# Merging and moving the copies of the held lookups, and layer 3 with its weight column stationary, in a recommendation tower

## The chip, the cores and the metric

The kernel runs on one core of a Trainium2 chip. The metric is the device time of one execution in microseconds (us), lower is better. Three executions of the kernel before took 525.3, 527.55 and 530.39 us; the median is 527.55 us.

## The reference

2048 samples each have a dense vector of 128 numbers and 26 indices, one into each of 26 tables of 128-number rows. Per sample the 27 vectors (dense and 26 looked up) are multiplied with each other in all 351 pairs. The products and the dense vector go through three layers:

```python
e = jnp.stack([tbl_0[ids[:, 0]], ..., tbl_25[ids[:, 25]]], axis=1)
combined = jnp.concatenate([dense[:, None, :], e], axis=1)          # (2048, 27, 128)
z = jnp.einsum('bfd,bgd->bfg', combined, combined)[:, IU0, IU1]      # 351 pairs
h = jnp.concatenate([dense, z, dense], axis=1)                       # (2048, 607)
h = jnp.maximum(h @ W_top1 + b_top1, 0.0)                            # 512 wide
h = jnp.maximum(h @ W_top2 + b_top2, 0.0)                            # 256 wide
y = h @ W_top3                                                       # 1 wide
```

## The kernel before

**Tiling.** The samples are worked in 8 pairs of tiles, `i` = 0 to 7, with 128 samples in each tile (`a` = 0 and 1). `PAIR` is 256 samples. The looked-up vectors come in two ways.

- 17 tables are gathered with indirect DMAs that POOL issues (L341), in five groups of 4, 4, 4, 4 and 1 tables, numbered `q` = 0 to 4. TensorE transposes each group (`turn`, L369) into one of two PSUM banks `p_turn`. ScalarE (ACT) copies it into `feats[a]` (`keep`, L580), and its semaphore count lets later turns go on. After a turn POOL may gather the same group of the next pair.
- 9 small tables lie in SBUF, split into a high and a low part. VectorE (DVE) makes a one-hot matrix for 256 samples (`make_onehot`, L713, a ring of three), and 16 matmuls pick the rows (`select`, L411). The result has 256 columns, one half for each tile of the pair, in `p_sel`. `keep_selected` (L603) copies 128 columns for each tile into `feats[a]`.

**Held selections.** Four of the nine selections of the next pair (k = 0 to 3, `HELD`) are made early, during the second half of the pair before, and stay in PSUM: two in each bank of `p_sel`. They can only be copied out once all products that read the old `feats[1]` are done, so the first copy waits for the last bank of `gram(i-1, 1)`. Selection k = 4 needs bank 0 free, so it waits for the copies of k = 0 and 1.

**Products.** `gram` (L433) computes the pair products of a tile in four banks of 16 fp32 matmuls; each shows as two matmul records, so a bank is 32 records. ACT copies each bank to `prods` (`keep_prods`, L618). SP stores `prods` to a DRAM buffer `square` in four DMAs (L203), waits for them to land, and reads the upper half back as `pairs_h` (L214, L217), the input of layer 1 (L448 and L454). Layer 2 is L491, layer 3 L503. DVE adds the biases and clips (L718, L723) and copies layer 3's result (L730).

**Order of the work.** All orders are written out by hand, one instruction stream for each engine, tied by semaphores. In pair `i`, TensorE does `turn(i,0,q)` for q = 0 to 4, with the last products of the pair before after q = 0 and 1 (two banks each), and the remaining selections k = 4 to 8 spread over q = 2 to 4 by the function `selections`. Then it turns the second tile, between which layers 1 to 3 of pair i-1, the products of tile 0 and the held selections of pair i+1 are placed. For TensorE pairs 2 to 6 are a loop, 0, 1 and 7 are written out. A last part does the final tile's products and the layers of the last pair by tile.

**Results.** `y` holds 16 columns of 128 samples in SBUF, filled two columns a pair, and goes out in one DMA at the end (L327).

Of the kernel before, what the change touches and what calls it, by code (L numbers as in the profile page):

```python
# [14 lines left out]
C = F + 1  # L15
# [59 lines left out]
def selections(q, first, second):  # L75
# [5 lines left out]
    start = 1 if second else 2  # L81
# [6 lines left out]
def place(k, first):  # L88


    return (k // 2, k % 2) if k < HELD and not first else (k % 2, 0)


def program(nc, x_t, ids, ids_t, tables, w_dense, w_pairs, b1, w2, b2, w3, out):
    ctx = ExitStack()
    with ctx:
# [39 lines left out]
        y = sb("y", [T, B // T])  # L136
        spare = sb("spare", [128, VC * D])

# [55 lines left out]
        s_out = sem("s_out")  # L194
# [28 lines left out]
        def _(sp):  # L223
# [71 lines left out]

            def pair(i, b, first=False, second=False, last=False, late=False):
                more = not (last or late)
                if not first:
                    store(i - 1, 1, first=second)
                if more and not first:  # L300
                    load_ids_part(i + 2, b, 0)
# [23 lines left out]

            sp.wait_ge(s_yr, NP + 1)
            sp.dma_start(out, y[:, :]).then_inc(s_out, 16)  # L327
            sp.wait_ge(s_out, 16)
# [29 lines left out]
        def _(pe):  # L358
# [137 lines left out]
            def layer3(u, own):  # L496

                for a in range(own.start // T, own.stop // T):
                    for k in range(M2):
                        if a == own.start // T and (k == 0 or own.stop - own.start == T):  # L500

                            pe.wait_ge(s_h2r, M2 * u + (k + 1 if own.stop - own.start == T else M2))
                        mm = pe.matmul(p_mlp[:, a:a + 1], h2[:, k, a * T:a * T + T], w3s[:, k:k + 1],  # L503
                                       start=(k == 0), stop=(k == M2 - 1))
                mm.then_inc(s_y, 1)
# [67 lines left out]
        def _(act):  # L573
# [18 lines left out]
            def keep_selected(i, k, first=False):  # L592

                f = C - 1 - k
                if k == 0 and not first:

                    act.wait_ge(s_gram, NG * 2 * i)
# [6 lines left out]
                ins.then_inc(s_fsel, 1)  # L604

# [15 lines left out]
            def pair(i, first=False, second=False):  # L621
# [7 lines left out]
                for q in range(NQ):  # L629
# [41 lines left out]
        def _(dve):  # L671
# [54 lines left out]
            def result(u, tile, own):  # L726

                own = slice(own.start // T, own.stop // T)
# [96 lines left out]
```

## Time and profile before

| | |
|---|---|
| median of three executions | 527.55 us |
| the profiled execution's own time | 527.54 us |
| its span in the trace | 525.4 us |
| mean granted TensorE clock | 0.86 of full |
| TensorE matmuls busy | 398.8 us (76%) |
| TensorE weight loads busy | 357.2 us (68%) |
| POOL busy | 260.7 us (50%) |
| DVE busy | 204.2 us (39%) |
| ACT busy | 160.5 us (31%) |
| DMA | 43.88 MB, 84 GB/s on the mean |

The span is what the trace shows from the first to the last instruction; about 2.1 us of the execution's time lie outside it. A busy share is an average over stages with different limits; what one change is worth has to be read in the stage where it acts. "Remote" or "another core or an unknown queue" as the end of a wait means that a semaphore moved at that moment, though no record of an instruction ends there. This kernel has only one core, so in its trace it is always a queue or a delay that has no record.

### The profile page before, as it was taken

The page shows a single profiled execution, that of the slowest core. Times are in us where ns is not written, and L with a number is a line of the kernel's source. Part 1 is how long each engine was busy: PE and PEld are TensorE (multiplying, and loading weights), DVE is VectorE, ACT ScalarE, POOL GpSimd, SP SyncE. Part 2 cuts the span into 40 slices and gives each one's busy share as a digit, 9 for nine tenths or more (in the row PEclk, how much of TensorE's full clock was granted, in tenths as well). Part 3 has the DMA queues.
Part 4 walks back from the last instruction along what each step waited for, and adds up shares of the span by engine and source line. Part 5 has one row for each costly group of instructions (what it writes and reads, how often), then busy time and mean ns, then how long its engine had stood idle before and what let it go on. Part 6 is the DMA issues. An engine that isn't in the chain of part 4 may idle for free.

```text
span 525.4 us, 9717 instructions
## 1 busy us (share of the span) xinstructions
PE 398.8 (76%) x3968; PEld 357.2 (68%) x3968; DVE 204.2 (39%) x157; ACT 160.5 (31%) x314; POOL 260.7 (50%) x278
## 2 busy tenths in 40 slices
PE   3641947674697689966897789955897588979997
PEld 2530846564586588955886578945886587868887
DVE  6110935553233434450533434450533532545103
ACT  0000543262222244214422333214421432226330
POOL 6774765645435654555546654565445653540000
PEclk9965877887898779978899679986999778979999
DMA  8981221743313152314414161313414140222031
GB/s 212 260 274 30 86 62 40 174 81 107 131 29 79 41 129 78 72 47 92 118 35 77 45 155 45 66 51 65 144 36 77 40 100 25 47 45 55 3 58 28
DMA packets 66355, 43.88 MB, mean 84 GB/s; under 512 B 51713, under 2 KB 56408, under 8 KB 66204
## 3 DMA queue, kind: packets, MB, share of 16 engines
q1 hardware_dynamic: 56068, 25.48, 20.1%
q0 software_dynamic: 8704, 17.84, 13.3%
q10 hardware_dynamic: 1560, 0.24, 0.3%
q8 instruction: 16, 0.26, 0.2%
q14 instruction: 7, 0.06, 0.0%
HBM read 37.78 MB, written 5.76 MB: 83 GB/s over the span
## 4 chain that ended last, share of the span: by engine, by line
PE 54%; another core or an unknown queue 26%; issue 7%; ACT 7%; DMA 3%; DVE 1%; ACTq 1%; SPq 1%; DVEq 0%
PE p_sel L411 24%; PE p_gram L433 9%; PE p_mlp L454 7%; PE p_turn L369 5%; PE p_mlp L491 3%; ACT feats L603 3%; ACT feats L580 3%; PE p_mlp L448 2%; DMA dense<-in_x_t 2%; PE p_sel L381 2%; ACT prods L618 1%; DMA square<-prods 1%; PE p_mlp L503 1%; DMA pairs_h<-square 1%
## 5 line engine op out<-in xcount | busy, mean ns | idle before, releaser
L341 POOL DMA_INDIRECT rows<-in_table,index x272 | 260.1, 956 | 208.2 <-PE p_turn L369 79.5
L713 DVE TENSOR_TENSOR onehot<-ids_all,p_rows 128x2048 fp32r<-128x2048 int32 x72 | 163.0, 2283 | 156.6 <-PE p_sel L411 83.8
L411 PE MATMUL p_sel<-onehot,high 125*128 125x256 f32 x528 | 153.4, 322 | 41.3 <-ACT feats L603 33.1
L411 PE MATMUL p_sel<-onehot,low 125*128 125x256 f32 x528 | 146.0, 308 | 1.8 <-issue 1.8
L411 PEld LDWEIGHTS p_sel<-onehot,high 125*128 125x128 f32 x528 | 114.9, 218 | 45.8 <-issue 25.6
L411 PEld LDWEIGHTS p_sel<-onehot,low 125*128 125x128 f32 x528 | 115.1, 218 | 3.2 <-issue 2.9
L580 ACT ACTIVATE feats<-p_turn 128x512 f32<-128x512 f32 (+1 forms) x80 | 79.6, 996 | 87.5 <-PE p_turn L369 49.2
L433 PEld LDWEIGHTS p_gram<-feats 128*54 128x54 f32 x2048 | 71.8, 156 | 50.5 <-issue 38.6
L433 PE MATMUL p_gram<-feats 128*54 128x52 f32 x2048 | 80.6, 241 | 33.1 <-ACT feats L580 17.3
L603 ACT ACTIVATE feats<-p_sel 128x128 f32<-128x128 f32 x144 | 44.6, 443 | 112.3 <-remote 65.5
L618 ACT ACTIVATE prods<-p_gram 118x416 f32<-118x416 f32 x64 | 33.4, 522 | 134.0 <-remote 93.7
L369 PE MATMUL p_turn<-ident,rows 128*128 128x128 f32 x272 | 51.5, 309 | 13.5 <-issue 13.5
L369 PEld LDWEIGHTS p_turn<-ident,rows 128*128 128x128 f32 x272 | 35.3, 157 | 17.2 <-issue 15.1
L454 PE MATMUL p_mlp<-pairs_h,weights 117*128 117x256 f32 x168 | 42.6, 391 | 0.0
L718 DVE TENSOR_SCALAR h<-p_mlp,b1s 128x256 f32<-128x256 f32 x28 | 13.5, 483 | 73.7 <-PE p_mlp L454 73.7
L454 PEld LDWEIGHTS p_mlp<-pairs_h,weights 117*128 117x128 f32 x168 | 33.0, 197 | 4.9
L491 PE MATMUL p_mlp<-h,weights 128*128 128x256 f32 x112 | 26.6, 380 | 0.2 <-DVE pairs_h L723 0.2
L381 PE MATMUL p_sel<-onehot,weights 125*128 125x256 f32 x48 | 13.5, 441 | 11.4 <-issue 11.4
L491 PEld LDWEIGHTS p_mlp<-h,weights 128*128 128x128 f32 x112 | 20.2, 190 | 2.6 <-issue 0.4
L723 DVE TENSOR_SCALAR pairs_h<-p_mlp,b2s 128x256 f32<-128x256 f32 x14 | 6.8, 484 | 35.1 <-remote 24.9
L381 PEld LDWEIGHTS p_sel<-onehot,weights 125*128 125x128 f32 x48 | 10.7, 225 | 13.4 <-issue 11.6
L448 PE MATMUL p_mlp<-dense,weights 128*128 (+1 forms) x56 | 17.4, 393 | 0.0
(46 smaller groups left out, 124.8 us busy)
## 6 DMA issues: line engine op xcount, KB each, us to landing
ids_all<-in_ids_t SPq DMA_DIRECT2D x25, 256.0 KB, 4.7
square<-prods SPq DMA_DIRECT2D x62, 87.8 KB
rows<-in_table,index POOLq DMA_INDIRECT x272
pairs_h<-square SPq DMA_DIRECT2D x14, 117.0 KB
weights<-in_table SPq DMA_DIRECT2D x3, 448.0 KB
prods<-in_table SPq DMA_DIRECT2D x3, 448.0 KB
ids_all<-in_ids_t SPq DMA_DIRECT2D x1, 1152.0 KB
ids_all<-in_ids_t SPq DMA_DIRECT2D x6, 128.0 KB
```

Of the source, the lines that this page charges most:

```text
L341: pool.indirect_dma_start(out=rows[a][:, f, :], out_offset=None, in_=tables[f], in_offset=bass.IndirectOffsetOnAxis(ap=index[:, (2 * i + a ...
L369: mm = pe.transpose(p_turn[(NQ * a + q) % 2][:, k * T:k * T + T], rows[a][:, f, :], ident[:, :])
L381: mm = pe.matmul(p_sel[k % 2][:, 0:PAIR], piece[k][0:VP, c, :], onehot[k % RING][0:VP, c, :].bitcast(F32), start=(c == 0), stop=(c == VC - 1))
L411: mm = pe.matmul(p_sel[bank][:, half * PAIR:half * PAIR + PAIR], part[k][0:VP, c, :], hot, start=(c == 0 and part is high), stop=(c == VC ...
L433: mm = pe.matmul(p_gram[b % 2][WIDE * tile:WIDE * tile + BLK, BLKC * k:BLKC * k + BLKC], group, feats[a][:, GB * b + k, js, 1:C], start=Tr ...
L448: pe.matmul(bank1(m, False)[:, 0:PAIR], wdense[:, cols], dense[:, bass.ds(i * PAIR, PAIR)], start=True, stop=False)
L454: mm = pe.matmul(bank1(m, False)[:, 0:PAIR], wpairs[:, c, cols], pairs[:, c, :], start=False, stop=(c == NCH - 1))
L491: mm = pe.matmul(bank2(m, tail)[:, 0:own.stop - own.start], w2s[:, k, 128 * m:128 * m + 128], h1[:, k, own], start=(k == 0), stop=(k == M1 ...
L580: nc.scalar.activation(dst, src, ACT.Copy).then_inc(s_feats, 1)
L603: ins = nc.scalar.activation(feats[a][:, :, :, f].rearrange("d g j -> d j g"), src, ACT.Copy)
L618: nc.scalar.activation(prods[a][0:RISE, :, GB * b:GB * b + GB], src, ACT.Copy)\
L713: nc.vector.tensor_tensor(onehot[k % RING][:, :, :], at, of, ALU.is_equal).then_inc(s_onehot, 1)
```

## The change

There are three edits.

1. **Selections and turns.** In pairs 2 to 7 the selections k = 4 to 8 start one group later (`start = 3` instead of 2): TensorE turns groups 2 and 3 back to back, then does k = 4 and 5, turns group 4, then k = 6 to 8.
2. **Copies of the held selections.** The two selections of a bank lie in swapped halves (`1 - k % 2`), so that their order in the bank is their order in `feats`, and one ACT instruction copies 2 x 128 columns of a tile. A bank takes two instructions (`keep_held`) instead of four. The copies of bank 0 now come before the copy of the last bank of products, and those of bank 1 right behind it, both ahead of group 2's copy.
3. **Layer 3.** The weight column `w3s` is the stationary operand and `h2` the moving one, so the result is one row of 256 numbers on one partition. `y` becomes a ring of two such rows in the memory of `spare`. SP stores each row when it is two pairs old (`store_y`), and DVE waits for that store before it writes the row again.

```diff
-    start = 1 if second else 2
+    start = 1 if second else 3
...
-    return (k // 2, k % 2) if k < HELD and not first else (k % 2, 0)
+    return (k // 2, 1 - k % 2) if k < HELD and not first else (k % 2, 0)
...
-        y = sb("y", [T, B // T])
         spare = sb("spare", [128, VC * D])
+        y = spare[0:1, 0:2 * PAIR]
...
+            def store_y(u, half):
+
+                sp.wait_ge(s_yr, u + 1)
+                sp.sem_inc(s_passed, 1)
+                sp.dma_start(out[:, bass.ds(u * PAIR, PAIR)], y[:, half * PAIR:half * PAIR + PAIR]).then_inc(s_out[half], 16)
...
                 if not first:
                     store(i - 1, 1, first=second)
+                if not (first or second):
+                    store_y(i - 2, b)
                 if more and not first:
                     load_ids_part(i + 2, b, 0)
...
-                for a in range(own.start // T, own.stop // T):
-                    for k in range(M2):
-                        if a == own.start // T and (k == 0 or own.stop - own.start == T):
-
-                            pe.wait_ge(s_h2r, M2 * u + (k + 1 if own.stop - own.start == T else M2))
-                        mm = pe.matmul(p_mlp[:, a:a + 1], h2[:, k, a * T:a * T + T], w3s[:, k:k + 1],
-                                       start=(k == 0), stop=(k == M2 - 1))
+                for k in range(M2):
+                    if k == 0 or own.stop - own.start == T:
+
+                        pe.wait_ge(s_h2r, M2 * u + (k + 1 if own.stop - own.start == T else M2))
+                    mm = pe.matmul(p_mlp[0:1, own], w3s[:, k:k + 1], h2[:, k, own],
+                                   start=(k == 0), stop=(k == M2 - 1))
...
+            def keep_held(i, bank):
+
+                f = C - 2 - 2 * bank
+                if bank == 0:
+
+                    act.wait_ge(s_gram, NG * 2 * i)
+                act.wait_ge(s_sel, SEL * i + 2 * bank + 2)
+                held = p_sel[bank].rearrange("d (f a j g) -> d f a j g", f=2, a=2, j=4)
+                for a in range(2):
+                    dst = feats[a][:, :, :, f:f + 2].rearrange("d g j f -> d f j g")
+                    ins = nc.scalar.activation(dst, held[:, :, a, :, :], ACT.Copy)
+                ins.then_inc(s_fsel, 2)
...
                     if not (first or second) and q < 2:
-                        keep_prods(i - 1, 1, range(NH * q, NH * q + NH))
-                    if not first and q == (0 if second else 1):
-                        for k in range(HELD // 2):
-                            keep_selected(i, k)
+                        keep_prods(i - 1, 1, (NH * q,))
+                        if q == 1:
+                            keep_held(i, 0)
+                        keep_prods(i - 1, 1, (NH * q + 1,))
+                        if q == 1:
+                            keep_held(i, 1)
+                    if second and q == 0:
+                        keep_held(i, 0)
                     if second and q == 0:
                         high_bits(5)
-                    if not first and q == (1 if second else 2):
-                        for k in range(HELD // 2, HELD):
-                            keep_selected(i, k)
+                    if second and q == 1:
+                        keep_held(i, 1)
...
-                nc.vector.tensor_copy(y[:, bass.ds(tile, own.stop - own.start)], p_mlp[:, own])\
+                nc.vector.tensor_copy(y[:, half * PAIR + own.start:half * PAIR + own.stop], p_mlp[0:1, own])\
                          .then_inc(s_yr, 1)
```

**How the instructions move.** ACT, in the loop over the pairs, from the last two copies of products (L618 before, L639 now; the held copies are L603 before and L624 now, a group's copy L580 and L591). Before:

```order
L618 ACTIVATE prods<-p_gram 118x52x8
L616 REGISTER_ALU
L618 ACTIVATE prods<-p_gram 118x52x8
L597 REGISTER_ALU
L598 ISA
L603 ACTIVATE feats<-p_sel 128x4x32 x2
L598 REGISTER_ALU
L603 ACTIVATE feats<-p_sel 128x4x32 x2
L577 REGISTER_ALU
L580 ACTIVATE feats<-p_turn 128x4x4x32
L598 REGISTER_ALU
L603 ACTIVATE feats<-p_sel 128x4x32 x2
```

Now:

```order
L639 ACTIVATE prods<-p_gram 118x52x8
L619 REGISTER_ALU
L620 ISA
L624 ACTIVATE feats<-p_sel 128x2x4x32 x2
L637 REGISTER_ALU
L639 ACTIVATE prods<-p_gram 118x52x8
L620 REGISTER_ALU
L624 ACTIVATE feats<-p_sel 128x2x4x32 x2
L588 REGISTER_ALU
L591 ACTIVATE feats<-p_turn 128x4x4x32
L588 REGISTER_ALU
L591 ACTIVATE feats<-p_turn 128x4x4x32
```

The first held copies went ahead of the last copy of products, and the copies of groups 2 and 3 now stand together.

TensorE, in its loop, from the last bank of products to group 4's single transpose. Before (the turns are L369, the selections L411):

```order
L433 MATMUL p_gram<-feats 54x52 x16
L367 REGISTER_ALU
L369 MATMUL p_turn<-ident,rows 128x128 x4
L393 REGISTER_ALU
L406 REGISTER_ALU
L411 MATMUL p_sel<-onehot,high 128x256
...
L367 REGISTER_ALU
L369 MATMUL p_turn<-ident,rows 128x128 x4
L393 REGISTER_ALU
L400 REGISTER_ALU
L411 MATMUL p_sel<-onehot,high 128x256
```

Now (the turns are L381, the selections L423):

```order
L445 MATMUL p_gram<-feats 54x52 x16
L379 REGISTER_ALU
L381 MATMUL p_turn<-ident,rows 128x128 x4
L379 REGISTER_ALU
L381 MATMUL p_turn<-ident,rows 128x128 x4
L405 REGISTER_ALU
L418 REGISTER_ALU
L423 MATMUL p_sel<-onehot,high 128x256
```

The turn of group 3 left its place between selections 4 and 5 and stands ahead of selection 4.

SP, in its loop: one DMA of 256 numbers is put between the four stores of products and the next load of indices.

```order
 L203 DMA square<-prods 702x1x32 x4
+L300 ISA
+L300 DMA out_y<-spare 1x256
 L238 ISA
 L241 ISA
```

Everything that SP issues behind it, the read-back of the products first, has one more DMA ahead of it in the queue.

## Rows read from the trace of the kernel before

**Rows 1.** The page, the chain that ended last, shares by engine.
```profile
PE 54%; another core or an unknown queue 26%; issue 7%; ACT 7%; DMA 3%; DVE 1%; ACTq 1%; SPq 1%; DVEq 0%
```

**Rows 2.** Stretches of pairs 2 to 7: length, busy us by engine, clock, DMA.
```profile
core 0: us, PE busy (x) PEld busy (x) DVE busy (x) ACT busy (x) POOL busy (x), PEclk, DMA share, GB/s
169.77:200.70 30.93, 22.12 (x227) 20.73 (x228) 12.09 (x7) 11.92 (x30) 16.98 (x18) 0.77 0.38 96
229.24:259.82 30.58, 23.67 (x236) 21.81 (x237) 12.26 (x7) 11.99 (x31) 16.97 (x18) 0.79 0.37 89
287.81:319.17 31.36, 24.22 (x227) 22.14 (x228) 12.09 (x7) 12.16 (x30) 16.98 (x18) 0.69 0.39 94
347.67:378.43 30.76, 21.78 (x227) 20.42 (x228) 12.04 (x7) 12.06 (x31) 16.97 (x18) 0.78 0.37 96
407.03:438.69 31.66, 22.54 (x226) 21.19 (x227) 12.20 (x7) 12.38 (x30) 16.99 (x18) 0.77 0.26 60
468.10:487.98 19.88, 18.32 (x227) 17.59 (x228) 11.32 (x6) 12.46 (x31) 0.94 (x1) 0.85 0.20 41
```

**Rows 3.** ACT's timeline in pair 5: start, us, line, [idle before it <- releaser].
```profile
362.15 0.52 ACT L618 ACTIVATE prods<-p_gram 118x416 f32<-118x416 f32 x1 [4.62 <-remote]
362.56 1.09 ACT L603 ACTIVATE feats<-p_sel 128x128 f32<-128x128 f32 x4
363.42 1.16 ACT L580 ACTIVATE feats<-p_turn 128x512 f32<-128x512 f32 x1
364.36 1.16 ACT L603 ACTIVATE feats<-p_sel 128x128 f32<-128x128 f32 x4
367.52 0.64 ACT L603 ACTIVATE feats<-p_sel 128x128 f32<-128x128 f32 x2 [1.99 <-PE p_sel L411]
...
374.80 0.63 ACT L603 ACTIVATE feats<-p_sel 128x128 f32<-128x128 f32 x2 [3.77 <-PE p_sel L411]
```

**Rows 4.** TensorE's timeline, the turn of group 2 in pair 5.
```profile
358.25 0.66 PE L369 MATMUL p_turn<-ident,rows 128*128 128x128 f32 x4
```

**Rows 5.** TensorE's timeline, the first matmul of selection 4 in pairs 2 to 6.
```profile
185.84 0.58 PE L411 MATMUL p_sel<-onehot,high 125*128 125x256 f32 x1 [4.68 <-ACT feats L603]
...
242.49 0.58 PE L411 MATMUL p_sel<-onehot,high 125*128 125x256 f32 x1 [3.00 <-ACT feats L603]
...
301.00 0.58 PE L411 MATMUL p_sel<-onehot,high 125*128 125x256 f32 x1 [2.14 <-ACT feats L603]
...
363.70 0.58 PE L411 MATMUL p_sel<-onehot,high 125*128 125x256 f32 x1 [4.79 <-ACT feats L603]
...
420.23 0.58 PE L411 MATMUL p_sel<-onehot,high 125*128 125x256 f32 x1 [3.02 <-ACT feats L603]
```

**Rows 6.** The chain in order of time: start, us, what.
```profile
363.70 3.78 PE p_sel L411 x16
367.48 0.85 PE p_turn L369 x4
...
488.15 1.30 PE p_mlp L454 x6
```

**Rows 7.** SP's timeline, reading back products: pair 5, then pair 7.
```profile
368.92 2.31 SPq L214 DMA_DIRECT2D pairs_h<-square  x3
...
481.61 2.25 SPq L214 DMA_DIRECT2D pairs_h<-square  x3
483.91 0.48 SPq L217 DMA_DIRECT2D pairs_h<-square  x1
```

**Rows 8.** Groups by line and form: busy us, mean ns of one, idle before.
```profile
L503 PE MATMUL p_mlp<-w3s,pairs_h 128*128 128x1 f32 x64 | 8.9, 256 | 10.9 <-issue 5.8 <-DVE pairs_h L723 5.2
L723 DVE TENSOR_SCALAR pairs_h<-p_mlp,b2s 128x256 f32<-128x256 f32 x14 | 6.8, 484 | 35.1 <-remote 24.9 <-PE p_mlp L491 10.2
L730 DVE COPY y<-p_mlp 128x2 f32 x4 | 0.6, 160 | 12.7 <-PE p_mlp L503 7.2 <-remote 5.5
```

**Rows 9.** DVE's timeline at the end of the program.
```profile
522.50 0.35 DVE L723 TENSOR_SCALAR pairs_h<-p_gram,b2s 128x128 f32<-128x128 f32 x1 [0.54 <-PE p_gram L491]
...
523.33 0.16 DVE L730 COPY y<-p_mlp 128x1 f32<-128x1 f32 x1 [0.47 <-PE p_mlp L503]
```

More of the change, by code:

```diff
@@ L193, in program @@
         s_yr = sem("s_yr")
-        s_out = sem("s_out")
+        s_out = [sem(f"s_out{half}") for half in range(2)]
         s_passed = sem("s_passed")
@@ L324, in _ @@
             read_back(NP - 1, (1,), chunks=(0, 1))
+            store_y(NP - 2, NP % 2)
             sp.wait_ge(s_yr, NP + 1)
-            sp.dma_start(out, y[:, :]).then_inc(s_out, 16)
-            sp.wait_ge(s_out, 16)
+            last = (NP - 1) % 2 * PAIR
+            sp.dma_start(out[:, B - PAIR:B], y[:, last:last + PAIR]).then_inc(s_out[(NP - 1) % 2], 16)
+            for half in range(2):
+                sp.wait_ge(s_out[half], 8 * NP)
         @block.gpsimd
@@ L594, in keep_selected @@
                 f = C - 1 - k
-                if k == 0 and not first:
-                    act.wait_ge(s_gram, NG * 2 * i)
                 act.wait_ge(s_sel, SEL * i + k + 1)
@@ L724, in relu2, with result @@
                                         b2s[:, m:m + 1], 0.0, ALU.add, ALU.max).then_inc(s_h2r, 1)
-            def result(u, tile, own):
-                own = slice(own.start // T, own.stop // T)
+            def result(u, half, own, stored=None):
+                if stored is not None:
+                    dve.wait_ge(s_out[half], 16 * stored)
                 dve.wait_ge(s_y, u + 1)
-                nc.vector.tensor_copy(y[:, bass.ds(tile, own.stop - own.start)], p_mlp[:, own])\
+                nc.vector.tensor_copy(y[:, half * PAIR + own.start:half * PAIR + own.stop], p_mlp[0:1, own])\
                          .then_inc(s_yr, 1)
@@ L744, in _, with pair @@
                 split_low(k)
-            def pair(i, b, second=False, last=False):
+            def pair(h, b, second=False, last=False, stored=True):
+                i = 2 * h + b
                 own = slice(0, PAIR)
@@ L768, in pair @@
                         make_onehot(i + 1, 1 - b, HELD - 1)
-                result(i - 1, 2 * (i - 1), own)
+                result(i - 1, 1 - b, own, h - 1 + b if stored else None)
             for k in range(HELD):
@@ L774, in _ @@
                 split_low(k)
-            pair(1, 1, second=True)
-            with dve.Fori(1, NP // 2 - 1) as h:
+            pair(0, 1, second=True, stored=False)
+            pair(1, 0, stored=False)
+            pair(1, 1)
+            with dve.Fori(2, NP // 2 - 1) as h:
                 for b in range(2):
-                    pair(2 * h + b, b)
-            pair(NP - 2, 0)
-            pair(NP - 1, 1, last=True)
+                    pair(h, b)
+            pair(NP // 2 - 1, 0)
+            pair(NP // 2 - 1, 1, last=True)
             for a in range(2):
@@ L786, in _ @@
                     relu2(NP - 1 + a, own, m, tail=True)
-                result(NP - 1 + a, 2 * (NP - 1) + a, own)
+                result(NP - 1 + a, (NP - 1) % 2, own, (NP - 1) // 2)
 def kernel(**inputs):
@@ L818 @@
           for k, a in arrays.items()}
-    out = nc.dram_tensor("out_y", (T, B // T), F32, kind="ExternalOutput").ap()
+    out = nc.dram_tensor("out_y", (1, B), F32, kind="ExternalOutput").ap()
     program(nc, ap["in_x_t"], ap["in_ids"], ap["in_ids_t"], [ap[f"in_table_{n}"] for n in range(F)],
@@ L823 @@
     r = run_bass_kernel_spmd(nc, [arrays], core_ids=[0])
-    return np.ascontiguousarray(r.results[0]["out_y"].T).reshape(B, 1)
+    return np.ascontiguousarray(r.results[0]["out_y"]).reshape(B, 1)
```

## The prediction, made before the changed kernel ran

> **What bounds the kernel now.** I read the chain that ended last first. TensorE holds 54% of it and ACT 7%, but 26% goes to "another core or an unknown queue" [rows 1]. With one core that can only be hidden waits: a semaphore moves late though no record ends there. So the kernel is bound by TensorE's order of work with its hand-overs, and a quarter of the chain is time that no instruction's record explains.
>
> Next I cut out the stage that the change touches. It runs from ACT's copy of group 4 of the second tile, after which the products of pair i-1 go on, to ACT's first copy of the second tile of pair i. The table of stretches has it for pairs 2 to 7 [rows 2]. In the loop pairs 2 to 6 it takes 30.93, 30.58, 31.36, 30.76 and 31.66 us, in pair 7, with the same work but no gathers (POOL 0.94 us busy against 17 us), 19.88 us. So some 11 us of each loop stretch are hidden waits or lower clock, and they are there only while POOL gathers. The five loop stretches differ by at most 1.1 us.
>
> The start of selection 4 in them is the most telling row [rows 5]. Counted from the stretch's start [rows 2], it comes at 16.07 us in pair 2 (185.84 - 169.77), 13.25 in pair 3, 13.19 in pair 4, 16.03 in pair 5 and 13.20 in pair 6. From there to the stretch's end it takes 14.86, 17.33, 18.17, 14.73 and 18.46 us. Pairs that start selection 4 2.8 us earlier get nothing for it: the rest grows by 2.5 to 3.7 us. The reader is to see that a head start before selection 4 has so far been taken back by a hidden wait behind it, such as the one before ACT's copy at 374.80 [rows 3].
>
> **The change part by part.**
>
> *Copies of the held selections.* Before, ACT copies the last bank of products at 362.15, the held bank 0 from 362.56 to 363.65, and selection 4 starts at 363.70 behind it [rows 3, 5]. Now bank 0 goes first, so it is free 0.41 us earlier (362.56 - 362.15). The merge itself I cost at nothing. Four copies of 128 columns take 363.42 - 362.56 = 0.86 us until the next instruction begins, and one copy of 512 takes 364.36 - 363.42 = 0.94 us [rows 3]. The same 512 columns cost the same in four instructions as in one, so two of 256 lie between, at 0.9 us.
>
> The Trainium skill says otherwise (VectorE: DVE Perf Modes, The TRN2 errata): each ScalarE instruction from PSUM pays 172 cycles at 1.2 GHz beside its columns, and few large ones are to be used. By that, an estimate, a bank would fall from 1.00 us (4 x 300 cycles) to 0.71 us (2 x 344), which gives 0.29 us more on the path of each pair, 1.7 us over six. The rows speak for no such gain, and the sum goes by them.
>
> So this part is worth 0.41 us in each of pairs 2 to 7, if it is kept. In the five loop pairs rows 5 say that a head start of 2.8 us is not kept, so I take 0 of 2.05 us there (both ends stay in the range). What it costs: the last bank of products is copied some 0.9 us later, and SP's stores with it; see the read-back below. The copies of bank 1 now stand ahead of group 2's copy, which delays that by 0.9 us. It is needed for group 4's turn, 8 us later, so nothing waits for it.
>
> *Turn of group 3 ahead of selection 4.* Before, TensorE turns group 2 at 358.25 to 358.91 and has nothing until 363.70 [rows 4, 5]. The turn of group 3 stands between selections 4 and 5 and takes 0.85 us of the chain (367.48 to 368.33) [rows 6]. It needs only the copy of group 1, long made, and rows gathered a pair ahead. So now it lies in the idle 4.8 us, and selection 5 follows 4 at once: 0.85 us less work behind selection 4. In the five loop pairs that is 4.25 us. Bounds: 0, if the hidden wait takes it as it took the head start, and 0.85 us a pair plus more, since POOL may gather group 3 earlier. I take the 0.85: this is TensorE work removed from behind selection 4, not an earlier start of it, and rows 5 say nothing against that kind. ACT has more to do before its copy of selection 4, about 0.9 + 0.4 + 0.9 + 0.9 + 0.9 = 4.1 us from the last gram bank (a held bank, a product bank, a held bank, two groups), while selection 4 ends 0.9 + 3.78 = 4.7 us after it [rows 3, 6]. So that copy is not late.
>
> *Pair 7.* Here there is hardly a hidden wait. Both parts would give some 0.8 us (0.41 and about 0.44, the turn at full clock being half of the 0.85). But layer 1 must find the products read back. SP issues that read-back at 481.61 to 484.39 [rows 7] and layer 1's matmuls on it start at 488.15 [rows 6], 3.8 us later, landing included. The read-back moves 0.9 us later with the product copy and could just become the last to arrive. I take 0.4 us.
>
> *Layer 3.* Each fp32 matmul shows as two records. Before it is 8 records a pair, starting about 0.12 us apart (1 column moved, 128 loaded). Now it is 4 records of 256 columns. The other fp32 matmuls of 256 columns start 0.217 us apart (1.30 us for six) [rows 6], so 0.87 us stands against 0.96. 0.1 us a pair less, and it ends beside ACT's late copy of group 4, so I take 0 of 0.7 us.
>
> *Result copy.* 128 x 2 takes 160 ns; a DVE operation with 256 columns from PSUM takes 484 ns [rows 8]. That is 0.32 us more a pair. Behind it on DVE is the one-hot of selection 4, made in 2.3 us some 13 us before it is needed: hidden. If that cover were gone it would be 2.3 us over 7 pairs. In the tail the last copy lies on the path: 0.35 us for 128 columns against 0.16 [rows 9], +0.19 us.
>
> *Stores of y.* One DMA of 1 KB a pair, issued by SP between the stores of products and the index loads. SP's issues cost 0.77 us each (2.31 us for three) [rows 7]. After the stores SP waits for them to land before the read-back, and this gap takes one more issue, so 0. Without the gap it would push the read-back by 0.77 us. SP's and DVE's new waits are for things 40 us or more old. The final DMA is 1 KB instead of 8 KB: 0.
>
> *Sum.* -4.25 - 0.4 + 0.19 = -4.46 us. The profiled execution took 527.54 us (span 525.4 and 2.1 around it), which is the median shown. 527.54 - 4.46 = **523.1 us**.
>
> **The rivals.**
>
> *All is kept, and more.* If the hidden waits are a fixed addition, each loop pair also keeps the 0.41 us (2.05 in all), pair 7 its other 0.4 and layer 3 its 0.1 a pair: 523.1 - 3.1 = **520.0 us**. POOL's earlier gathers can add to it. For it speaks that each hand-over is on the chain; against it rows 5.
>
> *All is taken back.* The loop stretches all end within 1.1 us of each other whatever happens in them [rows 2]. If something outside TensorE's order sets the hidden wait's end (gathers, stores or index loads, which pair 7 lacks), the 4.25 us come back as a longer wait: 527.54 - 0.4 + 0.19 = **527.3 us**. For it speaks that 2.8 us were taken back; against it that the hidden wait differs from pair to pair.
>
> *Slower: the read-back becomes the last to arrive.* The product copy is 0.9 us later, the y store adds 0.77 us in SP's queue if landing is shorter than now, and layer 1 is wanted up to 1.3 us earlier, so the read-back comes up to 3.0 us closer to its use. In pair 5 its first three issues end at 371.23 [rows 7], 7.2 us before the stretch's end at 378.43, in pair 7 it is 4.1 us (483.86 to 487.98). Taking 3.8 us as an upper bound of what it needs (pair 7, where it was in time), pair 5 has 3.4 us to spare. It decides from a shift above that. Should the hidden waits lengthen it so that each of the 6 pairs waits 1.5 us, the gain of 4.46 is lost and 9 us come on top: 523.1 + 4.5 + 9 = 536; with half of it, **532 us**. Little speaks for it in the loop.
>
> **How the numbers follow.** What a measurement of this kernel can tell from no change is about 1%, 5.3 us: faster means below 522.3, slower above 532.8. I give the forecast (523.1, with 2.5 us to either side) 0.38, all kept 0.22, all taken back 0.30, slower mechanism 0.10. Faster by over 1%: nearly all of the second case and four in ten of the first, 0.36. Slower by over 1%: somewhat over half of the last, 0.06. Within 1%: 0.58. The range takes in the kept case with POOL's extra down to 518.5, and the case taken back with the runs' own spread up to 529.5.
>
> **What would show it.** (1) In the stretches of rows 2, 0.8 us less in pairs 2 to 6 and some 0.4 less in pair 7. (2) TensorE turns group 3 within 1 us behind group 2, and selection 5 begins at selection 4's end. (3) ACT's two held copies of a bank take 0.85 to 0.95 us to the next instruction; 0.7 would show the page right. (4) Selection 4 starts 1.1 us instead of 1.55 us after the last gram bank is seen by ACT. (5) The result copy takes about 0.48 us, with no wait of SP or DVE for the y stores. Stretches still at 30.6 to 31.7 us with a longer idle time ahead of ACT's copies of selections 5 or 6 would show the gain taken back; a wait of layer 1 for the read-back would show the slower case. The prediction is wrong altogether if the hidden waits change by microseconds, which no row here explains.

## The result, and the profile after

The changed kernel is slower. Four executions took 541.26 to 548.08 us, median 544.89, beside 528.25 us for the kernel before (525.3 to 530.39, four executions). The ratio is 1.032, with a 95% interval of 1.023 to 1.040. The forecast was 523.1 us with a range up to 529.5, so the result lies outside it, on the other side of no change. The comparisons leave disturbed executions out. The profile below is of the slowest of the four, 548.08 us, with a span of 546.3 us.

The chain that ended last, shares by engine, of the changed kernel:

```profile
PE 48%; another core or an unknown queue 27%; issue 9%; ACT 8%; DMA 4%; SPq 1%; DVE 1%; ACTq 1%; DVEq 0%
```

TensorE's share fell from 54% to 48% [rows 1]. In microseconds the hidden waits went from 0.26 x 525.4 = 137 to 0.27 x 546.3 = 147, and "issue" (an engine that waits for nothing the trace shows) from 37 to 49. TensorE itself went from 284 to 262. All shares are rounded, and one point is 5 us. TensorE had no less to do: its matmuls are busy for 403.4 us, beside 398.8 before. So some 22 us left TensorE's part of the chain, and hidden waits and "issue" grew by some 23.

The same six stretches as [rows 2], cut at the same two copies of ACT:

```profile
core 0: us, PE busy (x) PEld busy (x) DVE busy (x) ACT busy (x) POOL busy (x), PEclk, DMA share, GB/s
173.49:207.64 34.15, 24.66 (x227) 23.28 (x228) 12.18 (x7) 11.70 (x27) 16.99 (x18) 0.70 0.34 87
236.16:270.15 33.99, 21.89 (x227) 20.82 (x228) 12.17 (x7) 11.87 (x26) 16.99 (x18) 0.80 0.33 87
298.66:335.32 36.66, 23.22 (x233) 20.57 (x232) 12.07 (x7) 12.07 (x26) 16.99 (x18) 0.73 0.32 80
362.15:399.09 36.94, 25.27 (x227) 23.48 (x228) 12.17 (x7) 12.13 (x26) 16.97 (x18) 0.68 0.33 82
427.61:460.90 33.29, 23.03 (x227) 21.44 (x228) 12.17 (x7) 12.01 (x26) 16.97 (x18) 0.74 0.25 57
489.26:507.05 17.79, 16.97 (x227) 16.25 (x227) 11.49 (x6) 12.20 (x27) 0.94 (x1) 0.91 0.21 45
```

The six together take 192.8 us against 175.2, which is 17.6 of the 20.9 us between the two spans. The five loop stretches are 1.6 to 6.2 us longer each, with nearly the same busy times of ACT, DVE and POOL. Pair 7, which has no gathers, got 2.1 us shorter, at a granted clock of 0.91 instead of 0.85. Where did the loop's time go? ACT's timeline in pair 5, the place of [rows 3]:

```profile
377.29 0.52 ACT L639 ACTIVATE prods<-p_gram 118x416 f32<-118x416 f32 x1 [7.55 <-remote]
378.12 1.12 ACT L624 ACTIVATE feats<-p_sel 128x256 f32<-128x256 f32 x2 [0.31 <-PE p_gram L445]
379.02 0.57 ACT L639 ACTIVATE prods<-p_gram 118x416 f32<-118x416 f32 x1
379.48 1.11 ACT L624 ACTIVATE feats<-p_sel 128x256 f32<-128x256 f32 x2
...
391.65 0.64 ACT L611 ACTIVATE feats<-p_sel 128x128 f32<-128x128 f32 x2 [7.69 <-remote]
392.07 0.45 ACT L591 ACTIVATE feats<-p_turn 128x128 f32<-128x128 f32 x1
392.31 0.69 ACT L611 ACTIVATE feats<-p_sel 128x128 f32<-128x128 f32 x2
```

TensorE meanwhile, first the turns, then the last two matmuls it did before the wait, and the first one behind it:

```profile
377.93 1.97 PE L381 MATMUL p_turn<-ident,rows 128*128 128x128 f32 x8
...
385.01 0.27 PE L381 MATMUL p_turn<-ident,rows 128*128 128x128 f32 x1
...
386.90 0.28 PE L423 MATMUL p_sel<-onehot,low 125*128 125x256 f32 x1
392.44 0.55 PE L423 MATMUL p_sel<-onehot,high 125*128 125x256 f32 x1 [5.26 <-ACT feats L611]
```

The turns of groups 2 and 3 stand together (x8), as the order says. Selection 5 ended at 385.2, group 4's turn at 385.3, selection 6 at 387.2. ACT takes up all three from 391.65 on, as if their signals came in one lot, 6.5 us late for the first. DVE starts its next one-hot at 391.65 too, after its own hidden wait of 6.07 us. And TensorE stands still for 5.26 us, since selection 7 needs the bank that ACT had not emptied. POOL's timeline shows what ran beside it, the first and last of a burst of eight indirect gathers, 1.25 us apart, and the next gather:

```profile
379.86 0.94 POOL L353 DMA_INDIRECT rows<-in_table,index  x1 [4.37 <-PE p_turn L381]
...
388.59 0.94 POOL L353 DMA_INDIRECT rows<-in_table,index  x1 [0.30 <-issue]
392.46 0.94 POOL L353 DMA_INDIRECT rows<-in_table,index  x1 [2.93 <-remote]
```

ACT goes on 2.1 us after the burst ends (391.65 - 389.53, the last gather's end, 388.59 + 0.94). So it is in every loop pair of the changed kernel: ACT's wait behind selection 4 ends 2.0, 2.1, 2.8, 2.1 and 1.2 us after a burst of 8, 8, 12, 8 and 8 gathers. The burst has this form because the turns of groups 2 and 3 now end together and free eight gathers at once; in pair 4 the four of group 1 ran into them. The kernel before, same engine, pair 5:

```profile
366.72 0.94 POOL L341 DMA_INDIRECT rows<-in_table,index  x1 [0.30 <-issue]
369.14 0.94 POOL L341 DMA_INDIRECT rows<-in_table,index  x1 [1.48 <-issue]
```

There the turns lay on both sides of selection 4, and so there were two bursts of four with a pause of 1.5 us. That was so in pairs 2 and 5; in pairs 3, 4 and 6 a burst of eight ran beside or right behind selection 4. These are the very pairs whose rest behind selection 4 was 17.3 to 18.5 us instead of 14.8 [rows 2, 5]. In the changed kernel selection 4 starts here in pairs 2, 3 and 6 (TensorE's timeline):

```profile
189.25 0.58 PE L423 MATMUL p_sel<-onehot,high 125*128 125x256 f32 x1 [3.59 <-ACT feats L624]
...
251.91 0.58 PE L423 MATMUL p_sel<-onehot,high 125*128 125x256 f32 x1 [4.03 <-ACT feats L624]
...
443.35 0.58 PE L423 MATMUL p_sel<-onehot,high 125*128 125x256 f32 x1 [3.13 <-ACT feats L624]
```

Counted from the stretch's start that is 15.8, 15.7 and 15.7 us, and the rest takes 18.4, 18.2 and 17.5. So these pairs now have the late start of the one kind (16.0 before) and the long rest of the other (17.3 to 18.5). Before, each pair had only one of the two.

The kernel before had such waits too, at another place: ahead of group 4's copy of the second tile, where the stretches of [rows 2] start. ACT waits there for 6.8 to 7.4 us in four of the six. In pair 2 a burst of eight gathers ends at 167.61, and ACT goes on 2.2 us later:

```profile
169.77 0.40 ACT L580 ACTIVATE feats<-p_turn 128x128 f32<-128x128 f32 x1 [7.41 <-remote]
```

So a wait of this size beside eight gathers could be read from the trace before the change, just outside the stretches that were cut out.

Layer 3 and the result copy, now (busy us, mean ns, idle before); then the tail's result copy:

```profile
L514 PE MATMUL p_mlp<-pairs_h,w3s 128*1 128x256 f32 x28 | 7.9, 410 | 8.2 <-issue 4.4 <-DVE pairs_h L747 3.8
L756 DVE COPY spare<-p_mlp 1x256 f32<-1x256 f32 x7 | 2.9, 412 | 30.4 <-remote 20.2 <-PE p_mlp L514 10.2
```

```profile
544.40 0.28 DVE L756 COPY spare<-p_mlp 1x128 f32<-1x128 f32 x1 [0.54 <-PE p_mlp L514]
```

Pair 7, SP's last read-back and the layer 1 that uses it:

```profile
502.88 2.29 SPq L214 DMA_DIRECT2D pairs_h<-square  x3
505.21 0.48 SPq L217 DMA_DIRECT2D pairs_h<-square  x1
```

```profile
508.93 1.56 PE L466 MATMUL p_mlp<-pairs_h,weights 117*128 117x256 f32 x6 [1.71 <-DMA pairs_h<-square]
```

Layer 1 waits 1.71 us for the read-back, which it did not before [rows 6, 7].

### The profile page after: what moved, and what is told of

Its sections match the earlier page's. It is cut to its first block, busy times and chain, and to the rows that moved or that the text cites. A ratio compares the mean times of both kernels' runs of the same rounds, so it can differ in the third digit from the quotient of the medians.

```text
span 546.3 us, 9595 instructions
## 1 busy us (share of the span) xinstructions
PE 403.4 (74%) x3940; PEld 355.6 (65%) x3940; DVE 205.8 (38%) x157; ACT 159.1 (29%) x286; POOL 259.5 (48%) x278
## 3 DMA queue, kind: packets, MB, share of 16 engines
q0 software_dynamic: 8704, 17.84, 12.7%
## 4 chain that ended last, share of the span: by engine, by line
PE 48%; another core or an unknown queue 27%; issue 9%; ACT 8%; DMA 4%; SPq 1%; DVE 1%; ACTq 1%; DVEq 0%
PE p_sel L423 18%; PE p_gram L445 10%; PE p_mlp L466 7%; PE p_turn L381 5%; ACT feats L591 4%; PE p_mlp L503 4%; PE p_mlp L460 2%; DMA dense<-in_x_t 2%; PE p_sel L393 2%; ACT feats L611 1%; DMA square<-prods 1%; DMA pairs_h<-square 1%; ACT prods L639 1%; ACT feats L624 1%
## 5 line engine op out<-in xcount | busy, mean ns | idle before, releaser
L423 PE MATMUL p_sel<-onehot,high 125*128 125x256 f32 x528 | 157.2, 327 | 56.7 <-ACT feats L611 31.0
L423 PEld LDWEIGHTS p_sel<-onehot,high 125*128 125x128 f32 x528 | 118.7, 225 | 60.5 <-issue 47.1
L423 PE MATMUL p_sel<-onehot,low 125*128 125x256 f32 x528 | 150.2, 314 | 0.6 <-issue 0.4
L423 PEld LDWEIGHTS p_sel<-onehot,low 125*128 125x128 f32 x528 | 118.5, 225 | 2.2 <-issue 1.9
L445 PE MATMUL p_gram<-feats 128*54 128x52 f32 x2048 | 81.5, 236 | 39.3 <-issue 27.2
L591 ACT ACTIVATE feats<-p_turn 128x512 f32<-128x512 f32 (+1 forms) x80 | 78.6, 999 | 86.3 <-PE p_turn L381 52.9
L639 ACT ACTIVATE prods<-p_gram 118x416 f32<-118x416 f32 x64 | 33.6, 525 | 131.0 <-remote 84.8
L611 ACT ACTIVATE feats<-p_sel 128x128 f32<-128x128 f32 x88 | 28.7, 438 | 122.9 <-remote 82.8
L381 PE MATMUL p_turn<-ident,rows 128*128 128x128 f32 x272 | 49.8, 307 | 12.6 <-issue 12.6
L381 PEld LDWEIGHTS p_turn<-ident,rows 128*128 128x128 f32 x272 | 34.7, 155 | 18.0 <-issue 15.0
L624 ACT ACTIVATE feats<-p_sel 128x256 f32<-128x256 f32 x28 | 15.7, 671 | 16.6 <-remote 16.0
```

The lines of the kernel that those rows point to most:

```text
L381: mm = pe.transpose(p_turn[(NQ * a + q) % 2][:, k * T:k * T + T], rows[a][:, f, :], ident[:, :])
L423: mm = pe.matmul(p_sel[bank][:, half * PAIR:half * PAIR + PAIR], part[k][0:VP, c, :], hot, start=(c == 0 and part is high), stop=(c == VC ...
L445: mm = pe.matmul(p_gram[b % 2][WIDE * tile:WIDE * tile + BLK, BLKC * k:BLKC * k + BLKC], group, feats[a][:, GB * b + k, js, 1:C], start=Tr ...
L591: nc.scalar.activation(dst, src, ACT.Copy).then_inc(s_feats, 1)
L611: ins = nc.scalar.activation(feats[a][:, :, :, f].rearrange("d g j -> d j g"), src, ACT.Copy)
L639: nc.scalar.activation(prods[a][0:RISE, :, GB * b:GB * b + GB], src, ACT.Copy)\
```

## The experiments

A "loop pair" below is the time from one copy of group 4 of the second tile to the next, in pairs 2 to 6. It is 58.6 to 61.1 us in the kernel before and 61.6 to 65.5 in the changed one.

### Which edit costs?

`e1_turns_only`: the kernel before with

```diff
-    start = 1 if second else 2
+    start = 1 if second else 3
```

> The kernel before with edit 1 alone (selections 4 to 8 one group later, turns of groups 2 and 3 back to back). Theory A (turns back to back let POOL issue eight gathers in one burst while selections 4 and 5 hand over, and TensorE's signals reach the others only at its end): carries most of the loss, 1.02 to 1.035 of before, with bursts of eight gathers in every loop pair and ACT's copy of selection 5 about 2 us after their end. Theory B (the copies or their order slow the stretch): about 1.00. Theory C (the result ring, its stores and waits): 1.00.

`e2_copies_and_layer3`: the changed kernel's other two edits, with `start` as before.

> The changed kernel with edit 1 undone (edits 2 and 3 alone). Theory A: 0.99 to 1.005 of before. Theory B or C: 1.02 to 1.035. Layer 3 and the result copy should be worth less than 0.5%.

`e3_after_pool_holds_group3` (on the changed kernel) and `e4_before_pool_holds_group3` (on the kernel before), the same three lines, so that the burst is parted:

```diff
+                            if a == 0 and q == 3 and i > 2:
+                                pool.wait_ge(s_sel, SEL * (i - 1) + 7)
+                                pool.sem_inc(s_passed, 1)
```

> The changed kernel; POOL alone is altered: it holds back the gathers of group 3 of the first tile (pairs 2 on) until selection 6 of the pair is done, so that the burst of eight is broken up. Theory A: the idle time ahead of ACT's copy of selection 5 falls from about 7 to under 4 us, and the time falls to 0.99 to 1.015 of before. Theories B and C: unchanged at about 1.03, or slower since POOL is held.

> The kernel before with the same hold of POOL. Before has bursts of eight in pairs 3, 4 and 6 only. Theory A: those pairs' stretches lose 2 to 3 us each, 0.98 to 0.995 of before. Otherwise 1.00, or slower since POOL starts four gathers later.

Measured, all four on one chip with the kernel before at 526.92 us: e1 543.97 us, ratio 1.027 (1.021 to 1.033). e2 544.61 us, 1.033 (1.029 to 1.037). e3 536.45, 1.020 (1.014 to 1.027). e4 537.78, 1.017 (1.013 to 1.022).

The turns alone cost as much as the whole change, and the two other edits alone do too, where theory A had them at nothing. The effects do not add up. In e1, ACT's wait behind selection 4 is 5.2 to 7.8 us in the five loop pairs, behind or beside bursts of eight and twelve. In e2 it is 5.7 to 5.9 us in pairs 3 to 5, the three that take 62.9 to 63.7 us (pairs 2 and 6 take 60.0 and 59.4), and there is no burst of eight there: two bursts of four, 0.9 to 1.2 us apart instead of 1.5. So eight gathers without a pause are not needed for the wait.

With POOL held (e3), the wait goes where the burst is parted. In pair 2 nothing hidden is left ahead of selection 5's copy:

```profile
196.78 0.67 ACT L614 ACTIVATE feats<-p_sel 128x128 f32<-128x128 f32 x2 [2.15 <-PE p_sel L426]
```

The idle time ahead of that copy is 1.9 us in pairs 3 and 5 and 2.8 in pair 6; in pair 4, where a burst of eight came about all the same, 4.8. The part of the pair up to group 4's copy of the first tile gets shorter (21.8 to 23.5 us instead of 26.7 to 29.9), and the rest longer (35.6 to 40.3 instead of 34.9 to 35.9). The gathers have to be made some time, and their cost moves with them. Nor does the time show a gain: e3's 1.020 is less than the 1.032 of the result, but the changed kernel itself had 1.017 on this chip at another time (e7 below). And the kernel before loses by the same hold. So the burst explains the place of the wait; that it explains the loss is not shown.

The two halves of e2, on another chip, whose times were unsteady: the kernel before took 518.46 to 538.93 us there, median 529.98. `e14_layer3_only` has edit 3 alone, `e15_copies_only` edit 2 alone.

> The kernel before with edit 3 alone (layer 3, ring of results, stores pair by pair). If any small shift of the work against the gathers costs: 1.005 to 1.035. If only the copies and turns do: 0.995 to 1.005.

> The kernel before with edit 2 alone (held copies merged and put ahead). Edits 2 and 3 together measured 1.033: this one takes what the run with edit 3 alone does not show, 1.00 to 1.03.

e14 took 528.66 us (518.41 to 530.48), like the kernel before. e15 took 535.77 (532.52 to 541.68). Layer 3 costs nothing that can be told; the copies seem to cost about 1% by the medians, 2.7% between the fastest executions, which four of each can't bound.

`e7_after_again` and `e8_before_on_this_chip` are the two kernels unchanged.

> The changed kernel once more, beside before on one chip. In the run without gathers, before itself took 380 us on the chip it was given, against 527 us elsewhere. If this call gets a chip of the 527 us kind: 1.025 to 1.04. If it gets one of the 380 us kind, where the hidden waits are missing, the forecast's own terms stand alone: 0.98 to 0.995. If the loss came from the change's order itself it would be slower on both.

> The kernel before, for a profile beside the others of this call. On a chip of the 380 us kind: no waits that end by remote over 2 us in pairs 2 to 6, stretches of 18 to 21 us, gathers at the same 1.25 us apart or faster. On one of the 527 us kind: stretches of 30 to 32 us as before.

e7 took 542.72 us, ratio 1.017 (1.008 to 1.025) to a kernel before of 532.34 us; e8, one execution, 527.34. The change is slower again, by a size that differs from chip to chip and time to time: 1 to 4% hold all of it.

### What makes the hidden waits?

`e5_after_no_gathers` and `e6_before_no_gathers` leave out the gathers of pairs 2 to 7 in either kernel, so the rows of pair 1 are used again.

```diff
-                        for f in quad:
+                        for f in quad if i < 2 else ():
```

> The changed kernel without the gathers of pairs 2 to 7 (left out with TensorE's waits on them; the rows of earlier pairs are used again). Theory A: the hidden waits go altogether, loop stretches of 17.5 to 21 us as in pair 7 instead of 33 to 37 us, time 0.80 to 0.88 of before. If the waits come from something else (instruction supply, the loop, the stores): stretches stay over 28 us.

> The kernel before without the gathers of pairs 2 to 7, in the same way. Theory A: like the changed kernel without them, and slower than that by 4 to 12 us, the forecast's terms (0.41 + 0.85 us a pair) and what pair 7 gained. If the order itself costs time: faster than the changed kernel without gathers.

e5 took 379.39 us and e6 377.97. But the kernel before itself took 380.12 us on that chip (376.59 to 383.29, 19 executions), with all its gathers. So these two told nothing of what the gathers cost on the chips above, and something else: there are chips on which the kernel before loses hardly anything by them (e6 has 0.997 of its time, 0.993 to 1.000). Theory A had e6 slower than e5 by 4 to 12 us. It was the faster, by 1.4. The stretch of [rows 2] takes 17.5 us in e5's loop pairs and 18.0 in e6's, so the change gains 0.5 us there, and the rest of the pair 24.1 to 24.5 us against 23.7, so it loses more behind it. Even without a gather the change is no gain. The next two were run on a chip where the kernel before takes 532.34 us.

`e10_pool_fills_no_dma`: the kernel before; in pairs 2 to 7 POOL fills the rows by memsets, without a DMA. `e11_plain_dmas_from_pool`: the same bytes come by plain DMAs that POOL issues. Neither gives the looked-up rows.

```diff
                         for f in quad:
+                            if i >= 2:
+                                pool.dma_start(out=rows[a][:, f, :], in_=tables[f][0:128, :]).then_inc(s_rows[a][q], 16)
+                                continue
```

> The kernel before; in pairs 2 to 7 each gather is replaced by eight POOL memsets of 16 columns of the same rows (about 0.9 us, no DMA). If POOL's instructions as such hold TensorE's signals back: like before on this chip. If it is the indirect DMAs, or their traffic: 0.71 to 0.75 of before on a chip of the 527 us kind (380 us); 1.00 on one of the other kind.

> The kernel before; in pairs 2 to 7 each gather is replaced by a plain DMA of 128 rows in a row of the same table, issued by POOL: same bytes, no index. If the traffic or POOL's part in issuing a DMA holds the signals back: within 3% of before on this chip. If it is the indirect form (128 descriptors from an index): 0.71 to 0.85 of before on a chip of the 527 us kind.

e10 took 420.65 us, ratio 0.792 (0.785 to 0.798), e11 425.13 (420.62 and 429.63). Every loop pair takes 41.7 to 42.5 us instead of some 60, and ACT has no hidden wait left in pairs 2 to 7 (those up to 106 us, in the first two pairs with their gathers, stay). In e11 the same queue moves the same 8704 packets and 17.84 MB as before. So neither POOL's being busy nor the traffic as such makes the hidden waits; something that comes with the indirect form does. A plain DMA differs from a gather in more than one way: it reads no index, its rows lie in a row, and it takes POOL 0.53 us instead of 0.94 and 0.30 of pause. Which of these counts was not tried.

`e12_after_plain_dmas` and `e13_before_plain_dmas`: the same replacement in both kernels, on the unsteady chip above.

> The changed kernel; in pairs 2 to 7 each gather is replaced by a plain DMA of the same bytes from POOL, as done to the kernel before. Theory A (the change loses only by what the indirect gathers do to the hand-overs): 0.98 to 1.00 of the kernel before with plain DMAs in the same call, with 0.4 to 1.3 us less a pair. Rival (the change's order costs by itself): 1.005 to 1.03 of it.

> The kernel before with plain DMAs in pairs 2 to 7, timed again beside the changed kernel with them. 0.79 to 0.82 of before on a chip of the 527 us kind, with pairs of 41 to 43 us.

e12 took 432.7 us (427.66 to 436.83), e13 425.11 (420.83 to 429.03). Without hidden waits in the loop the change is still no gain; it seems to lose 7.6 us by the medians, and 4.9 between the two profiled executions (427.66 and 422.77). One row of the waits of each (us in total, times, longest) shows where, e12 first:

```profile
PE p_mlp L469 <- DMA pairs_h<-square: 9.6, 6, 2.7
```

```profile
PE p_mlp L457 <- DMA pairs_h<-square: 0.9, 1, 0.9
```

In all six pairs layer 1 now waits for the read-back of the products.

### Does the number of gathers count, or their density?

`e16_before_spaced_gathers` puts eight small memsets between the kernel before's gathers, from pair 2 on. `e17_before_half_gathers` makes only the first two of each group of four (`quad[:2]`), so the other rows keep old values. `e18_after_once_more` is the changed kernel.

```diff
+                            if i >= 2:
+                                for n in range(8):
+                                    ins = nc.gpsimd.memset(gap[:, 96 * (f % 4) + 12 * n:96 * (f % 4) + 12 * n + 12], 0.5)
```

> The kernel before, with eight small memsets on POOL ahead of each indirect gather from pair 2 on, which puts about 0.35 us between gathers; all gathers are still made. If it is the density of a burst that delays TensorE's signals, the hidden waits shrink and the loop pairs fall from about 59.5 us towards 55, the whole by 10 us or more, to below 517 us. If each indirect gather delays them by itself, the sum is the same or a little larger (POOL needs 34 x 1.6 = 54 us a pair, below 59.5): 525 to 540 us.

> The kernel before, which from pair 2 on gathers only the first two tables of each group of four (18 of 34 gathers a pair); the other rows keep old values. If the delay goes with the number of indirect gathers, a loop pair takes 41.7 + 18/34 x 17.8 = 51 us, the whole about 480 us. If it is a matter of long bursts (eight and twelve in a row), bursts of two and four leave little of it: a pair below 46 us, the whole below 455.

> The changed kernel as it is, beside runs of the kernel before on the same chip. On a chip where the kernel before takes about 527 us: 537 to 548 us. On one where it takes about 380 us, the indirect gathers delay nothing, so the two kernels differ as they do without gathers: 378 to 382 us.

They came to another chip of the undelayed kind: the kernel before took 379.97 us (376.33 to 384.31, 13 executions). So the question stays open. e17 took 378.66 us, 0.998 (0.995 to 1.002). e16 took 431.89, 1.140 (1.131 to 1.148), and its chain has another head than all others:

```profile
POOL 52%; PE 24%; issue 9%; DMA 7%; DVE 4%; SPq 2%; ACT 1%; ACTq 0%; POOLq 0%; DVEq 0%
```

A gather with its pause takes 1.535 us there, 34 of them 52.2 us, and the loop pairs after the first take 51.3 to 53.9. POOL is the bound. Without the pause it is 34 x 1.25 = 42.5 us, and e18's loop pairs take 42.8 to 42.9 (44.9 in pair 6): POOL has next to nothing to spare.

e18 took 386.7 us (384.89 to 389.89), ratio 1.017 (1.009 to 1.026), where I had expected 378 to 382. This run has no hidden wait at all, so the loss can be looked for in plain waits. The chain of e18, then that of e6, the order of before on such a chip, though without gathers:

```profile
PE 61%; DMA 17%; SPq 9%; issue 5%; DVE 4%; ACT 3%; ACTq 1%; DVEq 0%
```

```profile
PE 79%; DMA 7%; DVE 4%; issue 4%; ACT 3%; SPq 2%; ACTq 1%; DVEq 0%
```

DMA and SP's queue went from 9% to 26% of it; in e17, which has the order of before and half the gathers on e18's own chip, they hold 11%. SP's timeline of one pair in e18, and TensorE's:

```profile
248.42 3.54 SPq L203 DMA_DIRECT2D square<-prods  x4
252.24 0.36 SPq L300 DMA_DIRECT2D out_y<-spare  x1
252.97 0.37 SPq L241 DMA_DIRECT2D ids_all<-in_ids_t  x1
254.91 2.32 SPq L214 DMA_DIRECT2D pairs_h<-square  x3
```

```profile
257.84 0.60 PE L381 MATMUL p_turn<-ident,rows 128*128 128x128 f32 x4
258.28 0.60 PE L460 MATMUL p_mlp<-dense,weights 128*128 x2
260.21 1.56 PE L466 MATMUL p_mlp<-pairs_h,weights 117*128 117x256 f32 x6 [1.33 <-DMA pairs_h<-square]
```

The last bank of products is copied later, behind the held bank, so the stores end later and the read-back starts later, while layer 1 is wanted no later. e18 loses 9.6 us in six such waits, e5 (no gathers) 2.4 in five, e17 0.4 in one. In e17's pair 5 the read-back starts 12.4 us after the stretch's start, in e18's 13.7. With all gathers the kernel before has no profile on such a chip, so how much of the 9.6 us it has too is not known.

SP's timelines of e6 and e5 at the same pair give the shift without the gathers. First e6, whose stretch starts at 236.68:

```profile
242.65 3.25 SPq L203 DMA_DIRECT2D square<-prods  x4
246.28 0.40 SPq L241 DMA_DIRECT2D ids_all<-in_ids_t  x1
248.54 2.31 SPq L214 DMA_DIRECT2D pairs_h<-square  x3
```

Then e5, whose stretch starts at 237.41:

```profile
244.67 3.19 SPq L203 DMA_DIRECT2D square<-prods  x4
248.14 0.36 SPq L300 DMA_DIRECT2D out_y<-spare  x1
248.88 0.36 SPq L241 DMA_DIRECT2D ids_all<-in_ids_t  x1
250.55 2.32 SPq L214 DMA_DIRECT2D pairs_h<-square  x3
```

Counted from the stretch's start, the stores begin after 7.26 us instead of 5.97, and the read-back after 13.14 instead of 11.86: 1.28 us. The y store itself adds nothing: SP still waits for the stores to land behind it.

## Why the prediction was wrong

**The step that failed** is in the sum: "I take the 0.85: this is TensorE work removed from behind selection 4 ... and rows 5 say nothing against that kind." It priced the turn of group 3 as TensorE work only. A turn also frees a group of gathers, and moving it changed when POOL makes them. The forecast said of this only that POOL's earlier gathers "can add to" the gain. Edit 1 alone costs 17 us by the medians (e1), and 14 by its ratio of 1.027, where -4.25 stood. The zero for the copies and layer 3 in the loop failed in the same way: these two edits without the turns cost as much (e2, 17.7 us). In both runs ACT's hidden wait behind selection 4 is over 5 us in the pairs that lose. That the edits raise hidden waits is shown; that they do it by moving the gathers is argued from where the bursts lie. The prediction had named the risk, hidden waits that change by microseconds, and the rows to see it in: in all of [rows 2] the 11 us were there only where POOL gathered. I read that as a fixed sum to be kept or taken back, and in the one rival with a loss as a thing that only lengthens the read-back, never as a sum that the edit itself could raise.

**Rows 5, half right.** That an early selection 4 gained nothing was true, but the reading, a head start taken back, was incomplete. The pairs with the early start were those in which the gathers of two groups had run together. The change made that the rule in all five. POOL's own timeline would have shown the bursts before.

**The rivals.** All kept (520.0) and all taken back (527.3) fell. The slower rival (532) had the right sign and, on the chips that this result is from, the wrong place: layer 1 waits for the read-back only once there, 1.7 us in pair 7. On the undelayed chip and with plain DMAs it is what happens, six waits and 9.6 us in all. That this is near the 9 us it named is luck: it got them from a landing lengthened by hidden waits, which these runs don't have, and the whole loses 6.7 and 7.6 us there. Where there are hidden waits, layer 1 comes late itself and the read-back is in time. It deserved more than a chance of 0.10, since its margin in pair 7 was the thinnest number of the prediction.

**The smaller terms.**
- Merged copies: right. Two copies of 256 take 0.90 us to the next instruction (378.12 to 379.02), against 0.86 for four of 128 and 0.94 for one of 512 [rows 3]. By the rule of the Trainium skill (VectorE: DVE Perf Modes, The TRN2 errata) it would be, an estimate, 0.71 us; these rows don't agree with it. (The forecast's "2 x 344" should read 2 x 428 cycles; its 0.71 us is right.)
- Pair 7: forecast -0.4. From group 4's copy to group 4's copy it takes 36.25 us instead of 36.37: the stretch is 2.1 us shorter, the rest 2.0 longer, 1.7 of it layer 1's wait. In e5 and e6 the same stretch differs by 0.5 us (17.60 and 18.07), so most of the 2.1 is not the edits' work; the clock was higher.
- Layer 3: forecast a gain of 0.1 us a pair, at nothing. Without delays, ACT's copy of the turn behind it comes 1.54 us after the stretch's start in e5 (238.95) and 1.28 in e6 (237.96): a loss of 0.26 us a pair.
- ACT's work ahead of its copy of selection 4: the forecast's sum of 4.1 us is 4.0.
- Result copy: forecast 0.48 us, measured 0.41; in the tail 0.28 instead of 0.35. No wait for the y stores, as said.
- Selection 4 behind the last bank of products: forecast 1.1 us after ACT sees that bank and starts on the held one, measured 1.15 in pair 2 (ACT's copy at 188.10, selection 4 at 189.25). The 0.4 us are there. In pair 5 they are not: the products themselves ended late, at 378.0, so the two turns lay on the path (to 379.9) and not in an idle time.

**What stays open.** Why TensorE's work is taken up late beside indirect gathers on some chips and not on others, and what in a gather does it. How the two groups of edits each raise the hidden waits by as much as all three together. The records can't tell late signals from late instructions: the same chips show more "issue" in the products too, 13.0 us ahead of TensorE's product matmuls before and 27.2 after the change, none in e6 and e18. Whether the number or the density of gathers counts was not settled. And there is no profile of the kernel before from a chip where it takes 380 us.

## What to carry to other kernels

A moved step takes with it everything that it releases. Ask of a turn not only what it costs its engine but which DMAs its signal lets loose, and beside which hand-overs they will run. When a quarter of the chain is waits with no record and they occur only beside one resource, draw that resource's timeline first; a forecast in tenths of a microsecond has no ground there. And a step that delays the producer of a store that is read back is paid at the read-back: find the pair with the least margin and take it as the rule.

## What the runs showed of the hardware

- Two kinds of chips. The kernel before took 518 to 539 us on some and 376 to 384 us on two others. Of the experiments' chips only one was used at two different times (527 and 532 us), so that it is the chip, and not the time, is not settled. With plain DMAs or memsets in place of the indirect gathers of pairs 2 to 7, this kernel takes 419 to 430 us on the first kind (e10, e11, e13), and its loop pair 41.7 to 42.8 us, nearly the same as on the second kind without gathers (41.7, e6).
- On the first kind, ACT, DVE and POOL take up TensorE's work late, by 6.5 us in the rows above and 9.4 in pair 4 of the changed kernel. Behind a burst of eight or more gathers the wait mostly ends 1.8 to 2.8 us after the burst. Beside bursts of four ACT's waits are shorter and end nearer: in the kernel before at 205.46 and 213.47, 3.6 and 3.9 us long, 0.5 us before the burst's end, and at 184.29, 4.7 us long, 1.0 us after it. On the second kind nothing of the sort is seen, though in e18 POOL gathers every 1.25 us with hardly a pause.
- An indirect gather of 128 rows takes POOL 0.94 us and the next starts 1.25 us after its start. 34 of them a pair are 42.5 us, whatever the tiles' work.
- The granted clock goes with it: 0.85 and 0.86 in the profiles of both kernels on the first kind, 0.93 and 0.95 in e10 and e11, 0.97 to 0.99 in e18, e5 and e6.
